# A column Haar tree for the synthesis, attended values turned by DMA, and new written orders for five engines

## The reference

```
3 levels of a 2-D Haar transform; every band is scaled by a gate
    (softmax of 3 / sigmoid, computed from the image), then the inverse transform
h = concat(cls_token, image rows)            # 257 tokens of 256 features
h = h + attention(layernorm(h))              # 16 heads of 64, rotary, causal with ALiBi
h = h + ffn(layernorm(h))                    # int8-rounded tokens, ternary weights, inner size 1024
```

## Time and profile before

| | us |
|---|---|
| median of 3 runs | 1755.23 (1753.16 to 1758.5) |
| span of the profiled execution | 1750.5 |
| PE busy | 1664.2 (95%) |
| DVE busy | 1470.0 (84%) |
| ACT busy | 1323.6 (76%) |
| POOL busy | 1120.1 (64%) |

### The profile page before, as it was taken

The page is one execution under the profiler, slowest core; times in us unless marked ns, Lnnn a source line. Parts: engine busy times, 40 slices in busy tenths (PEclk is TensorE's granted clock), DMA queues, the critical chain, the costliest instruction groups (busy, mean ns, idle before and its releaser), DMA issues.

```text
span 1750.5 us, 48653 instructions
## 1 busy us (share of the span) xinstructions
PE 1664.2 (95%) x16742; PEld 1278.3 (73%) x16742; DVE 1470.0 (84%) x4972; ACT 1323.6 (76%) x3812; POOL 1120.1 (64%) x1034
## 2 busy tenths in 40 slices
PE   7758999999999999999999999999999999999975
PEld 6635777777777777777777777777777777777653
DVE  3837888899888888899888888899888888889874
ACT  0326888888888888888888888888888888888762
POOL 0087667766777666766777667666677667666500
PEclk9789999999999999999999999999999999999986
DMA  9311111111111111111111111111111111111100
GB/s 320 110 61 61 56 53 56 53 67 57 61 68 68 59 61 57 50 65 62 56 68 68 66 55 60 54 56 66 55 64 68 68 53 61 56 53 62 44 7 13
DMA packets 90168, 113.70 MB, mean 65 GB/s; under 512 B 14818, under 2 KB 52163, under 8 KB 89667
## 3 DMA queue, kind: packets, MB, share of 16 engines
q1 hardware_dynamic: 89922, 110.59, 18.1%
HBM read 26.62 MB, written 8.42 MB: 20 GB/s over the span
## 4 chain that ended last, share of the span: by engine, by line
PE 88%; DVE 4%; SPq 3%; POOL 2%; ACT 1%; issue 1%; DMA 0%; DVEq 0%; POOLq 0%; ACTq 0%
PE bank L725 45%; PE bank L842 9%; PE bank L983 7%; PE bank L831 6%; PE bank L829 6%; PE bank L994 3%; PE bank L853 3%; PE bank L903 3%; PE bank L891 2%; PE bank L1003 2%; SPq L320 1%; PE bank L882 1%; DVE arena L1283 1%; PE bank L950 0%; POOL rot L486 0%
## 5 line engine op out<-in xcount | busy, mean ns | idle before, releaser
L482 POOL TENSOR_TENSOR arena<-rq,cos 128x512 f32<-128x512 f32 x256 | 326.1, 1274 | 280.0 <-ACT rq L526 280.0
L535 ACT ACTIVATE arena<-arena,nm 128x129 f32<-128x129 f32 (+1 forms) x1024 | 455.6, 455 | 0.0
L486 POOL TENSOR_TENSOR rot<-rot,sin 128x512 f32<-128x512 f32 x256 | 326.3, 1275 | 103.9 <-DMA rot<-rq 103.9
L725 PE MATMUL bank<-xt_h,weights 128*128 128x256 f16 x2048 | 378.9, 273 | 9.2 <-ACT rq L526 7.8
L526 ACT ACTIVATE rq<-bank,bqk 128x256 f32<-128x256 f32 x512 | 214.4, 471 | 170.1 <-PE bank L725 155.3
L1283 DVE CUSTOM_DVE_ANT_0 arena<-bank,bias 128x129 f32<-128x129 f32 (+1 forms) x1024 | 317.9, 352 | 26.5 <-issue 16.6
L489 POOL TENSOR_TENSOR arena<-arena,rot 128x512 f32<-128x512 f32 x256 | 314.2, 1228 | 37.3 <-POOL rot L486 0.9
L1291 DVE TENSOR_TENSOR ptr_l<-bank,ptr_h 128x384 f16<-128x384 f32 x512 | 280.0, 552 | 31.8 <-ACT ptr_h L545 29.4
L545 ACT ACTIVATE ptr_h<-bank 128x384 f16<-128x384 f32 x512 | 249.1, 486 | 68.6 <-PE bank L725 44.0
L725 PE MATMUL bank<-xt_l,weights 128*128 128x256 f16 x1024 | 279.6, 273 | 0.0
L842 PE MATMUL bank<-eye,arena 128*128 128x128 f32 x1536 | 253.0, 277 | 8.5 <-DVE ptr_l L1291 4.4
(11 more groups left out here) (200 smaller groups left out, 3182.5 us busy)
## 6 DMA issues: line engine op xcount, KB each, us to landing
rot<-rq SPq DMA_DIRECT2D x512, 128.0 KB, 2.0
arena<-in_x SPq DMA_DIRECT2D x4, 2048.0 KB, 15.2
xin<-in_x SPq DMA_DIRECT2D x32, 256.0 KB, 2.8
hr<-hr SPq DMA_DIRECT2D x32, 256.0 KB, 2.3
out<-h SPq DMA_DIRECT2D x64, 128.0 KB, 2.1
arena<-in_L_attn_w_qkv SPq DMA_DIRECT2D x2, 1536.0 KB, 8.6
weights<-in_L_ffn_w_down SPq DMA_DIRECT2D x1, 1024.0 KB, 11.8
arena<-in_L_ffn_w_gate SPq DMA_DIRECT2D x1, 1024.0 KB, 8.5
```

The source lines that it names most:

```text
L482: pool.tensor_tensor(dst, rq[:, g % 2].rearrange("p j (t n) -> p j t n", t=T), cos[:, :].rearrange("p (t n) -> p t n", t=T).unsqueeze(1).b ...
L486: pool.tensor_tensor(r, r, sin[:, :].unsqueeze(1).broadcast_to([P, 2, SIDE]), ALU.mult).then_inc(t2_ready, 1)
L535: act.activation(cols, cols, ACT.Exp, bias=nm[:, t, h:h + 1], scale=-1.0, accum_out=rs[:, t, h:h + 1]).then_inc(e_done, 1)
L725: ins = pe.matmul(dst, lhs[l], rhs[r], start=start and n == 0, stop=stop and n == len(parts) - 1)
```

## The change

**Synthesis.** POOL now makes a column tree of sums and differences (`column_bands`: tile `haar`, 512 columns = 256 differences, 128, 64, and 64 sums). PE applies the four row operators to the four parts, 256 + 128 + 64 + 64 columns, into one bank; `coarse` is gone. ACT copies all 512 columns out (`synthesis_out`), and POOL undoes the tree in six operations (`image_back`), the last of which gives `h_ready`. `project(s,5)` waits for the copy (`syn_out_done`).

**Attended values.** ACT takes the high half of `ao` from SBUF, POOL subtracts for the low half, and SP turns both by DMA (`dma_start_transpose`, fp16, 128x512 each, 8 a step). `out_transposes` and DVE's `attended_lo` are gone; `attention_out` waits for the DMAs.

**Smaller edits.** The row patterns and gate factors of the preparation are fewer operations over 16 instead of 12 terms. The `ve` operation of `norm_stats` becomes two of one column each. `hr_moved` becomes two semaphores. POOL's rotary work is three separate calls (`cosine`, `sine`, `turned_sum`).

```diff
             def synthesise(a):
...
-                pe.matmul(b_bank[:, :], rowop[:, 0, :], xin[:, :, :].rearrange("p t n -> p (t n)"), start=True, stop=True).then_inc(syn_ready, 1)
-            def coarse(a):
...
-                for o, (src, n) in enumerate(((s1, 128), (s2, 64), (s3, 32))):
...
-                    ins = pe.matmul(u_bank[:, 0:SIDE], rowop[:, o + 1, :], rhs, start=o == 0, stop=o == 2)
+                for o, (dst, src) in enumerate(zip(columns(b_bank), columns(haar))):
+                    ins = pe.matmul(dst.rearrange("p t n -> p (t n)"), rowop[:, o, :], src.rearrange("p t n -> p (t n)"), start=True, stop=True)
+                ins.then_inc(syn_ready, 1)
...
+            def image_back(a):
+                pool.wait_ge(syn_out_done, a + 1)
+                pool.tensor_tensor(quad_sum[:, :, 0::2], low, d3, ALU.add)
+                pool.tensor_tensor(quad_sum[:, :, 1::2], low, d3, ALU.subtract).then_inc(back, 1)
+                pool.wait_ge(back, 2 * a + 1)
+                pool.tensor_tensor(pair_sum[:, :, 0::2], quad_sum[:, :, :], d2, ALU.add)
+                pool.tensor_tensor(pair_sum[:, :, 1::2], quad_sum[:, :, :], d2, ALU.subtract).then_inc(back, 1)
+                pool.wait_ge(back, 2 * a + 2)
...
+                pool.tensor_tensor(hh[:, :, 0::2], pair_sum[:, :, :], d1, ALU.add)
+                pool.tensor_tensor(hh[:, :, 1::2], pair_sum[:, :, :], d1, ALU.subtract).then_inc(h_ready, 1)
...
+            def column_step(low, high, src):
+                pool.tensor_tensor(high, src[:, :, 0::2], src[:, :, 1::2], ALU.subtract)
+                return pool.tensor_tensor(low, src[:, :, 0::2], src[:, :, 1::2], ALU.add)
+            def column_bands(first):
+                d1, d2, d3, low = columns(haar)
+                column_step(s1[:, :, :], d1, xin).then_inc(coeffs, 1)
+                pool.wait_ge(coeffs, first)
+                column_step(s2[:, :, :], d2, s1).then_inc(coeffs, 1)
+                pool.wait_ge(coeffs, first + 1)
+                column_step(low, d3, s2)
             def attended_hi(c, g):
-                act.activation(at_h[:, :, 2 * g:2 * g + 2, :], pt_bank[u % 2][:, :].rearrange("p (t j n) -> p t j n", t=T, j=2), ACT.Copy).then_inc(hi_done, 1)
+                act.activation(ao_h[:, g % 2], ao[:, g % 2].rearrange("p t n -> p (t n)"), ACT.Copy).then_inc(at_hi, 1)
...
+            def attended_lo(c, g):
+                pool.tensor_tensor(ao_l[:, g % 2], ao[:, g % 2].rearrange("p t n -> p (t n)"), ao_h[:, g % 2], ALU.subtract).then_inc(at_lo, 1)
...
+            def turn_attended(c, g):
+                sp.wait_ge(at_lo, 4 * c + g + 1)
+                if c and g < 2:
+                    sp.wait_ge(op_ready, c)
+                for dst, src in ((at_h, ao_h), (at_l, ao_l)):
+                    sp.dma_start_transpose(dst[:, g].rearrange("p t j n -> p (t j) n"), src[:, g % 2]).then_inc(at_in[g % 2], 16)
...
             def attention_out(e, p):
                 if p == 0:
-                    pe.wait_ge(pt_free, at_use(e - 1, 2) + 1)
+                    pe.wait_ge(at_in[0], 64 * e)
+                    pe.wait_ge(at_in[1], 64 * e - 32)
                 if p == 1:
-                    pe.wait_ge(pt_free, at_use(e - 1, 3) + 1)
+                    pe.wait_ge(at_in[1], 64 * e)
```

More of the change, by code:

```diff
@@ L82, in pt_use @@
 def pt_use(c, h):
[L84 to L89 removed]
+    return 16 * c + h
 def vit_layer(nc, x, cls_tok, Wa, ba, Wd1, bd1, Wd2, bd2, Wd3, bd3, w_qkv, b_qkv, w_out, b_out,
@@ L709, in step @@
                 input_hi(s + 2)
-                weights_hi(s, 14)
-                exps(s, 15)
-                attended_hi(s, 2)
-                exps(s + 1, 0)
-                to_rotate(s + 2, 0)
             for s in range(-4, IMAGES + 6):
@@ L1020, in step @@
             def step(s):
+                turn_inner(s - 2, 1)
+                transposes(s - 1, 3)
                 scores(s - 1, 3)
+                project(s, 2)
                 down(s - 2, 1)
-                out_transposes(s - 2, 3)
-                values(s - 1, 0)
-                values(s - 1, 1)
+                values(s - 1, 2)
+                values(s - 1, 3)
+                transposes(s - 1, 4)
                 attention_out(s - 1, 0)
-                transposes(s - 1, 3)
+                transposes(s - 1, 5)
                 attention_out(s - 1, 1)
@@ L1040, in step @@
+                values(s - 1, 7)
+                transposes(s - 1, 8)
+                project(s, 5)
                 turn_tokens(s - 1)
-                values(s - 1, 4)
-                values(s - 1, 5)
-                out_transposes(s - 1, 0)
-                project(s, 5)
-                scores(s - 1, 5)
+                transposes(s - 1, 9)
+                scores(s - 1, 6)
                 gate_up(s - 1, 0)
-                transposes(s - 1, 7)
                 project(s, 6)
-                transposes(s - 1, 8)
+                values(s - 1, 8)
@@ L1080, in step @@
+                turn_input(s + 1)
+                values(s - 1, 14)
+                scores(s, 2)
+                values(s - 1, 15)
+                transposes(s, 1)
                 project(s + 1, 0)
-                transposes(s - 1, 15)
+                transposes(s, 2)
                 down(s - 1, 0)
-                values(s - 1, 14)
                 project(s + 1, 1)
-                transposes(s, 0)
-                scores(s, 2)
-                project(s + 1, 2)
-                transposes(s, 1)
@@ L1089, in step @@
-                turn_inner(s - 1, 1)
-                transposes(s, 2)
-                values(s - 1, 15)
+                values(s, 0)
+                values(s, 1)
             for s in range(-4, IMAGES + 6):
@@ L1327, in norm_stats @@
                 chain.settle()
-                ts(shifted[:, :], agg[:, :, 1], 1e-5, None, ALU.add).then_inc(ready, 1)
+                for t in range(T):
+                    ins = ts(shifted[:, t:t + 1], agg[:, t, 1:2], 1e-5, None, ALU.add)
+                ins.then_inc(ready, 1)
             def centre_tokens(ep):
@@ L1486, in step @@
             def step(s):
-                image_out(s - 1)
                 evict_scores(s - 3, 8)
                 evict_scores(s - 3, 9)
-                weights_lo(s - 3, 6)
-                image_stats(s - 1)
+                weights_lo(s - 3, 7)
+                token_scales(s - 3)
+                reciprocals(s - 3, 1)
                 evict_scores(s - 3, 10)
-                attended_lo(s - 3, 0)
+                evict_scores(s - 3, 11)
+                normalise(s - 3, 1)
+                weights_lo(s - 3, 8)
```

451 lines of the change are left out of this document (218 added, 233 removed).

## The result

| | before | after |
|---|---|---|
| median of 11 runs each, us | 1753.16 (1749.74 to 1758.5) | 1741.21 (1737.94 to 1751.77) |
| span of the profiled execution | 1750.5 | 1743.0 |

The ratio is 0.9935 [0.9922, 0.9949]: faster by 0.65%, where 4% was forecast. 12 us were gained instead of 70.

The account below looks back on a forecast made before the run. PE alone was taken to bound 29.1 steps of 49.06 us; at 46.5 a step 74.5 us go, and with +4 for the edges and 4.7 from span to median this gave 1685 us, own range 1666 to 1705 (overall 1660 to 1745).

Parts of the forecast that it names:

- PE's own work: PE's step: 49.06 less 1.30 for `coarse` and 1.76 for `out_transposes`, plus 0.04 for the synthesis, gives 46.04 us.
- The floor of 0.11 a record: Synthesis on PE: a small fp32 record costs about 0.11 us however few its columns, two records a product.
- Rival 2: Synthesis on PE: short fp32 products cost as much as long ones, +0.6 us, 1702; upper end of the forecast's 0.53.
- Neither binds by its sum: DVE and ACT per step: 40.3 and 41.5 us of work in 46.0, so neither was to bind.
- the split of `ve`: DVE: splitting the `ve` operation was to move 0.2 us a step either way.
- I allow 0.45 us a step for all these near misses: 46.5: PE's waits at `project 5`, `scores 6` and similar places: 0.45 us a step in all, making the step 46.5.
- Rival 4: Near misses in five rewritten orders eat the saving: about 3 us of waits a step, 1755 us; chance 0.04.
- One for one, until another engine takes over: Steady part: work taken off PE shortens the step by as much, until another engine or a wait takes over.
- POOL: POOL per step: 43.7 us of work plus 1.1 for operations awaiting their predecessor, 44.8 of 46.0, 97%.
- The transposing DMAs: Attended values ahead of `attention_out`: landing taken as about 3 us, with 4.5 to 5.5 left for two issues and landing.
- rival 3: Transposing DMAs land late, at `attention_out`: a loss from over 8 us after issue, 1816 at 10; chance 0.15.
- Edges: Preparation and last image: `image_back(0)` ahead of the first statistics and a longer path for the last attended values, +4 us.

Follow-up runs that it names:

- e1: Changed kernel with the two normalise_image operations (`xn`) in the tensor_scalar form that also writes an accumulator, factor rstd left out: 1706.7 us.
- e5: Changed kernel with the normalisation `xn` moved from DVE to ACT, DVE making only -mean*rstd, nothing left out: 1695.7 us.
- e8: Kernel before with 2.2 us a step of PE work left out and `ve` written as one-column operations: 1722.3 us.
- e3: Changed kernel with plain DMAs of the same size in place of the eight transposing ones, the turn left out: 1734.9 us.
- e4: Kernel before without three of four `out_transposes` of each group and two of three `coarse` products, 2.2 us of PE's step: 1737.2 us.
- e11: Changed kernel with `xn` on ACT, and 8 of the 16 `down` products of PE left out: 1683.1 us.
- e2: Changed kernel with POOL's eight sine products a step on 128 of their 256 columns: 1727.2 us.
- e6: Changed kernel with `xn` in the accumulator form (rstd left out) and POOL's sine products on half their columns: 1704.8 us.
- e7: Changed kernel with the four subtractions for the attended low halves moved from POOL back to DVE: 1819.2 us.

## Why the prediction was wrong

- **PE's own work.** Right in size: 46.04 was forecast without losses, 49.06 - 2.86 = 46.2 measured. The four products take 1.27 us from the first to the next matmul, not 1.1: the one of 256 columns 0.52 where 0.43 was taken, the other three 0.75 where 0.66 was, and the latter holds the 0.09 by which `scores` starts late. The floor of 0.11 a record held: records of 128 and 64 columns are 0.06 to 0.11 apart. Rival 2 had priced the four at 1.73.
- **"Neither binds by its sum".** This is one of the two steps that failed. DVE's share was read as a price, 0.41 for each `xn`, that would hold in any surroundings. The sum was nearly right (40.3 us a step forecast, 433.96 / 511 x 49.07 = 41.7 measured, with the 1.34 of waiting in it), but of the two operations of 0.4 us one became 1.35 and the other 0.8 at the place in the order on which PE's transposes hang. e1 and e5 show it: 1.3 to 1.6 us of the mean step (1.1 to 1.5 of the median one), 35 to 45 us. The rows ahead of the prediction carried half of the warning: POOL waited for `rq` once a step, 9.1 us, and the new order puts work there. What DVE does in that gap was never asked, though the spread of `ve` (168 to 1256 ns) stood in the trace. For the same reason the split of `ve`, put at 0.2 us either way, saved DVE 2 x 0.537 - 4 x 0.149 = 0.48 us a step, and was worth 0.47 in e8.
- **"I allow 0.45 us a step for all these near misses: 46.5".** The other step that failed: they are 2.9. Of these 1.1 to 1.5 are DVE's wait above (by the median steps of e1 and e5), 0.26 the long steps that vanish with the transposing DMAs (e3), and 1.1 to 1.5 stay open. Rival 4 named this size (about 3 us a step, 1755 us), with a chance of 0.04 and no place where it would be lost.
- **"One for one, until another engine takes over".** e4 refutes it for the old order, by 0.58 of 2.2 us, and e11 for the new. Here a PE that was busy for all of the window had DVE right behind it, whose own share was 89%.
- **POOL.** Its sum held: 44.8 us a step forecast with its own waits; 43.4 busy (452.28 / 511 x 49.07) and 5.2 waiting measured, and it did not bind (e2, e6). `attended_lo` took 1.16 (forecast 1.27); `image_back` took 3.0 and not 2.6, since the two interleaving operations of 256 columns take 0.73 each and not 0.615, and the two of 128 columns 0.46 and not 0.40:

```profile
L558 POOL TENSOR_TENSOR ao_l<-ao,ao_h 128x512 f16<-128x512 f32 x104 | 120.5, 1159 | 69.0 <-ACT ao_h L636 69.0
...
L500 POOL TENSOR_TENSOR hh<-pair_sum,syn 128x256 f32<-128x256 f32 x26 | 19.0, 731 | 0.0
...
L493 POOL TENSOR_TENSOR pair_sum<-quad_sum,syn 128x128 f32<-128x128 f32 x26 | 11.9, 457 | 2.0
```

- **ACT.** `attended_hi` from SBUF took 0.63 (0.75 forecast), the copy of the synthesis 0.57 (0.60).
- **The transposing DMAs.** Landing 2.5 to 2.6 us, near the 3 taken; rival 3 needed 8. PE waited for them four times in 26 steps, 2.3 us. What wasn't counted is that each holds SP for 1.2 to 1.3 us, twice a plain one.
- **Edges.** +4 us was forecast. The first synthesis of the steady part is where it was (306.12 against 306.13), and the draining is 7.8 us shorter, the whole gain of the profiled execution.

The Trainium skill has the rule that the prediction lacked, on its page "SBUF — State Buffer", section "Who interferes with whom": VectorE in a 2-port mode (a `tensor_scalar` can enter one, the form that also writes its accumulator cannot) and a GpSimd operation exclude each other for a whole instruction, and whoever issued first makes the other wait. By the same section a VectorE instruction with two inputs in SBUF contends with a GpSimd one that reads SBUF. This case agrees in what it shows: 52 of 52 `xn` at a mean of 1077 ns beside POOL, 408 without; 473 with the accumulator; in e7 waits in both directions for two inputs in SBUF. That `xn` runs in a 2-port mode is taken from the page; no run here shows the mode itself.

## What to carry to other kernels

A duration from a trace holds for what ran beside it. Before an order is rewritten so that GpSimd fills its idle time, list the VectorE operations in that stretch with all operands in SBUF (a wide min-to-max spread gives them away), and move them to ScalarE or use a form that doesn't wait; here the first gained nearly four times what the whole change did (45.5 against 12 us). And a TensorE that is busy all the time says nothing of how far the next engine is behind: leave out some of its work in a run before pricing a saving one for one.

## What the runs showed of the hardware

- A VectorE `tensor_scalar` of 256 fp32 columns in SBUF takes 0.408 us alone and up to 1.445 beside GpSimd (1.544 in e7); it ends 0.15 us after the GpSimd operation that was in progress. The `ve` operation of two columns waits as well (up to 1.284), that of one column doesn't (0.156 at most), nor do the form with the accumulator (0.478), ScalarE's (0.594) and the subtraction that reads one operand from PSUM (0.560).
- The wait goes both ways with two VectorE inputs in SBUF (e7): VectorE's 0.68 became up to 1.78, GpSimd's 1.27 became 1.71.
- A `scores` matmul (fp32, 64 rows) starts 0.093 us later than another would, whatever 128-row matmul stands ahead of it.
- A transposing DMA of 128x512 fp16 holds its queue for 1.20 to 1.27 us (medians of the high and the low half) and lands after 2.5 to 2.6; the plain one 0.51 to 0.60 and 2.0 to 2.1. The Trainium skill's page "Advanced Engine Details and Errata", section "X-Bar Transpose (TRN2)", has them as fast as plain ones: by these rows they land 0.5 us later.
